# Cross-attention with an FFN on one core: V computed straight in rows for two head groups at once, and a slot's value products in one piece

## Chip, cores, metric

One NeuronCore of one Trainium2 chip runs the whole kernel in one launch. The metric is the device time of the launch in microseconds (us), median over runs. TensorE (PE in the rows) multiplies, VectorE (DVE), ScalarE (ACT) and GpSimd (POOL) work element by element, SyncE (SP) issues most DMAs.

## The reference, cut

For 32 batches of 64 rows of width 512, with H = 32 query heads, 8 key/value heads (groups), D = 128:

```python
q = (layernorm(x) @ Wq).reshape(nb, 64, 32, 128)     # k, v likewise from ctx, with 8 heads
q, k = rope(q), rope(k)                              # cos/sin rows gathered by position
k, v = repeat(k, 4), repeat(v, 4)                    # 4 query heads share a group
attn = softmax(where(mask == 0, -1e9, q @ k.T / sqrt(128)))
x = x + (attn @ v).reshape(nb, 64, 4096) @ Wo
# FFN: router softmax over 8 experts gives in_scale and out_scale per row
xf = layernorm(x)
x = x + (xf * in_scale @ sign(weight).T * out_scale + bias)
```

All inputs and results are float32. The kernel keeps that precision on TensorE by splitting each operand into a part `hi`, rounded to fp32r, and the rest `lo`, and multiplies hi·hi + hi·lo + lo·hi: three matmuls for each product of 128 rows.

## The kernel before

**Slots.** The 2048 rows make 16 tiles of 128 rows (two batches), taken in 4 quarters of 4 tiles (512 columns when transposed). For each quarter the 8 groups follow one another. A slot does, at the same time, the projections of its own group U (K, four Q heads, V: `project(s, 0..5)`), the attention of the group before (scores, softmax, values) and the output projection of the group before that (`out_proj(s, 0..3)`, one for each tile). There are 32 such slots (slot 0 only projects, slot 1 has no output projection), then `attend_last` and a last stage. Beside this, some slots take in a tile of the next quarter (transposes of context, positions and x: an *intake* slot; g = 2 to 5 of the first quarter, g = 0, 1, 6, 7 of the second and third), and slots g = 2 to 5 of the later quarters run the FFN of a finished tile (an *FFN* slot). What is neither is a *plain* slot. Of the even slots 2 to 30, six are FFN slots, six intake slots, three plain.

**Order.** Every engine runs its own list, written out by hand (`slot(s)` in each engine's block); semaphores tie them. Nothing is scheduled by a planner. A projection is 12 matmuls with 512 columns moving (`split_products`, L1129: 4 chunks of 128 by three products), the weights stationary. TensorE's order in a slot before: `out_proj 0`, V's transposes, scores, `out_proj 1, 2, 3`, `project 0`, transposes of the probabilities (`probs_T`), `project 1`, `values 0`, `project 2`, `project 3`, `values 1`, `project 4`, `project 5`, with the small steps of intake and FFN between them.

**V before.** `project(s, 5)` gives V of the group transposed (columns are rows of the context). ScalarE copies it to `vT` (`v_out`, L605); in the next slot `v_rows` (L1161) turns it with four TensorE transposes into `V_BANK`, ScalarE and VectorE split it into `v_hi` (`v_in_rows`, L571) and `v_lo` (`v_lo_split`, L846).

**Values.** `values(s, d)` (L1192) multiplies V with the transposed probabilities of two tiles (a *duo*): 12 matmuls of 64 rows by 256 columns, always two at a time in the two halves of the array. Both duos write the same two banks `o_ps`, so `values 1` waits until `out_hi` (ScalarE) and `out_lo` (VectorE) have emptied them, and stands two projections later.

**Weights.** A group's K, Q, V and Wo chunks (10 in a slot, 256 KB each) come through a ring of five raw buffers in the order `STREAM`; ScalarE makes `hi` (`split_hi`, L553), GpSimd makes `lo` (`split_lo`, L413), and `wsplit_lo` counts them. `w_hi`, `w_lo` hold three chunks (`WRING`).

**Rotary embedding.** After a projection j (0 is K, 1 to 4 are Q heads) VectorE's `rotate(s, j)` (L860) makes two half products with sin into `swp` and one with cos, and GpSimd's `rope_sum(s, j)` (L424) adds them. `cos_done` frees the PSUM bank of the projection, `roped` lets the scores of the next slot begin.

Of the kernel before, what the change touches and what calls it, by code (L numbers as in the profile page):

```python
# [26 lines left out]
def attention_ffn(nc, x, ctx_in, pos, mask, wq, wk, wv, wo, ffn_w, ffn_bias, gate_w, in_scale, out_scale,  # L27
# [26 lines left out]
    STREAM = [0, 1, 2, 3, 6, 4, 7, 5, 8, 9]  # L54
    FIRST_STREAM = [0, PROJ - 1, 1, 2, 3, 4]
# [11 lines left out]
    with stack:  # L67
# [16 lines left out]
        vT = sb("vT", [P, BT])  # L84
        v_hi, v_lo = (sb(n, [P, PAIRS, D], F32R) for n in ("v_hi", "v_lo"))
# [5 lines left out]
        pT_hi, pT_lo = (sb(n, [P, 2, 2 * P], F32R) for n in ("pT_hi", "pT_lo"))  # L91
# [6 lines left out]
        c_tile, x_tile, f_tile, fT = (sb(n, [P, E]) for n in ("c_tile", "x_tile", "f_tile", "fT"))  # L98
# [22 lines left out]
        xs_hi, xs_lo = sb("xs_hi", [P, E], F32R), sb("xs_lo", [P, E], F32R)  # L121
# [4 lines left out]
        in_raw, out_raw, gate_raw = probs[:, 0, :], probs[:, 1, :], c_tile  # L126
# [3 lines left out]
        sc_ps, tr_ps, aux = (stack.enter_context(nc.psum_tensor(n, [P, 512], F32)) for n in ("sc_ps", "tr_ps", "aux"))  # L130
        o_both = stack.enter_context(nc.psum_tensor("o_ps", [P, 2, 512], F32))
        o_ps = [o_both[:, i, :] for i in range(2)]

        DUO_BANK, V_BANK, TABLE_BANK = [sc_ps, tr_ps], o_ps[0], o_ps[1]
        C_BANK, X_BANK = [aux, sc_ps, tr_ps, o_ps[0]], [chunk[2], o_ps[1], sc_ps, aux]
        ROWS_BANK, SGN_BANK, GATE_BANK = [tr_ps, o_ps[0]], [o_ps[0], sc_ps, tr_ps, aux], o_ps[1]
        x_first = [x_tile, f_tile, fT, y]
# [28 lines left out]
        PROJ_BANK = [1, 2, 0, 1, 2, 1]  # L166
# [16 lines left out]
        vT_ok, v_tr, v_h, v_ok = sem("vT_ok"), sem("v_tr"), sem("v_h"), sem("v_ok")  # L183
# [21 lines left out]
        class Slot:  # L205


            def __init__(self, q, g, ffn, intake, residual=False):
                self.q, self.g = q, g
                self.U = q * KVH + g  # L210
# [8 lines left out]
                self.ffn, self.intake, self.residual = ffn, intake, residual  # L219
                side = q % 2  # L220
# [10 lines left out]
        def run_slots(eng, slot, last_step, newest_first=False):  # L231


            quarter(eng, slot, 0, False, True)
            with eng.Fori(1, QT - 1) as q:
                quarter(eng, slot, q, True, True)
            quarter(eng, slot, QT - 1, True, False)
            slot(last_attention)
            last_slot = Slot(QT, 1, False, False)
            for turn in range(PAIRS + LAST_STEPS - 1):  # L240
                tiles = [p for p in range(PAIRS) if 0 <= turn - p < LAST_STEPS]
                if newest_first or turn < PAIRS:
                    tiles.reverse()
                else:
                    tiles.sort(key=lambda p: turn - p == PRODUCT_STEP)
                for p in tiles:
                    last_step(last_slot, turn - p, p)

        def quarter(eng, slot, q, has_ffn, has_intake):
# [5 lines left out]
            with eng.Fori(TJ, TJ + PAIRS) as g:  # L255
                slot(Slot(q, g, has_ffn, first, has_intake))
            with eng.Fori(TJ + PAIRS, KVH) as g:
                slot(Slot(q, g, False, has_intake and not first))
# [5 lines left out]
        def jobs_of(s):  # L264
# [3 lines left out]
            t = tile_in(s, i if s.residual else s.g if isinstance(s.g, int) else s.g - PAIRS) if s.intake else None  # L268
# [3 lines left out]
        def loads_of(s):  # L272

            return FIRST_STREAM if s.first_proj else STREAM if s.proj else [PROJ + h for h in range(HG)]

        def ring_use(s, n):

            return (n % RING, n // RING + 1) if s.first_proj else ((n - HG) % RING, 2 * s.U + (n - HG) // RING + 1)

        def split_count(s, n):  # L280

            return n + 1 if s.first_proj else s.U * CH - HG + n + 1

        def rank(s, j):

            return FIRST_STREAM.index(j) if s.first_proj else j

        def proj_bank(s, j):

            return chunk[0 if s.first_proj and j == PROJ - 1 else PROJ_BANK[j]]  # L290
# [19 lines left out]
        def heads_of_o(p):  # L310
            return o_both[:, :, bass.ts(p % 2, HG * S)].rearrange("p b (h s) -> p b h s", h=HG)
# [9 lines left out]
        def flat2(buffer):  # L321
            return buffer[:, :, :].rearrange("p b n -> p (b n)")
# [9 lines left out]
        def _(sp):  # L332
            def load_tile(t):

                sp.wait_ge(c_tr, t)
                sp.dma_start(c_tile[:, :], row_of(ctx_t, t)).then_inc(c_in, 16)
                sp.wait_ge(x_tr, t)
                sp.dma_start(x_tile[:, :], row_of(x_t, t)).then_inc(x_in, 16)

            def load_weights(s):  # L340
                for n, c in enumerate(loads_of(s)):
                    r, _ = ring_use(s, n)
                    if c >= PROJ:
                        grp = (s.g + KVH - 1) % KVH if isinstance(s.g, int) else s.g - 1
                    else:
                        grp = s.g
                    if not (s.first_proj and n < RING):
                        sp.wait_ge(wsplit_lo, split_count(s, n) - RING)
                    if c < PROJ:
                        src = (wk_c[:, :, bass.ts(grp, D)] if c == 0 else  # L350
                               wv_c[:, :, bass.ts(grp, D)] if c == PROJ - 1 else
# [4 lines left out]
                    if s.first_proj and n == 0:  # L356
# [21 lines left out]
            def slot(s):  # L378
                if s.intake:
                    load_tile(jobs_of(s)[0][0])  # L380
# [20 lines left out]
        def _(pool):  # L401
# [11 lines left out]
            def split_lo(s, n):  # L413
# [3 lines left out]
                if c < PROJ:  # L417
                    hi, lo = (flat(w[:, rank(s, c) % WRING, :, :]) for w in (w_hi, w_lo))
# [39 lines left out]
            def first_projections(s):  # L458
                second = Slot(0, 1, False, False)
                for n in range(3, PROJ):  # L460
                    split_lo(s, n)
                    rope_sum(s, n - 3)
                split_lo(second, 0)
                rope_sum(s, KQ - 2)
                split_lo(second, 1)
                rope_sum(s, KQ - 1)

            def slot(s):
# [13 lines left out]
                if s.proj:  # L482
                    split_lo(s, 3)
                    split_lo(s, 4)
                    rope_sum(s, 0)
                    rope_sum(s, 1)
                    split_lo(s, 5)
                    split_lo(s, 6)
                    split_lo(s, 7)
                    rope_sum(s, 2)  # L490
                if s.ffn:
                    xs_lo_split(f[0], in_slot)
                if s.proj:
                    rope_sum(s, 3)
                    split_lo(s, 8)
                    split_lo(s, 9)
                    rope_sum(s, 4)
# [29 lines left out]
            def first_quarter():  # L527
# [4 lines left out]
                split_lo(first, 0)  # L532
                split_lo(first, 1)
                pool.wait_ge(consts, 1)
                pool.wait_ge(x_st3, PAIRS)
                nc.gpsimd.tensor_tensor(s_rstd[:, :], s_var[:, :], half[:, :], ALU.pow).then_inc(x_st4, PAIRS)
                split_lo(first, 2)
                wait_alone(pool, rows_tr, PAIRS)
                nc.gpsimd.memset(scores[:, :, :], MASKED).then_inc(fill_ok, 1)

# [5 lines left out]
        def _(act):  # L546
# [6 lines left out]
            def split_hi(s, n):  # L553
# [3 lines left out]
                if c < PROJ:  # L557
                    k = rank(s, c)
                    if not (s.first_proj and k < WRING):
                        act.wait_ge(proj_done, s.U * PROJ + k - WRING + 1)  # L560
                    hi = flat(w_hi[:, k % WRING, :, :])
# [9 lines left out]
            def v_in_rows(s):  # L571
                act.wait_ge(v_tr, s.U)
                if not s.first_attn:
                    act.wait_ge(pv_done, (s.U - 1) * DUOS)
                copy(flat2(v_hi), V_BANK[:, :]).then_inc(v_h, 1)

            def exp_duo(s, d, part=range(8)):
# [3 lines left out]
                if not s.first_attn:  # L581
                    act.wait_ge(probs_tr, n - 1)
# [6 lines left out]
            def pT_hi_split(s, d):  # L589
# [3 lines left out]
                if not (s.first_attn and d == 0):  # L593
                    act.wait_ge(pv_done, n)
                copy(flat2(pT_hi), DUO_BANK[d][:, :]).then_inc(pT_h, 1)
# [8 lines left out]

            def v_out(s):  # L605
                act.wait_ge(proj_done, s.U * PROJ + rank(s, PROJ - 1) + 1)
                if not s.first_proj:
                    act.wait_ge(v_tr, s.U)
                copy(vT[:, :], proj_bank(s, PROJ - 1)[:, :]).then_inc(vT_ok, 1)
# [847 lines left out]
```

## Time and profile before

| | us |
|---|---|
| median of 3 runs (1177.56 to 1177.73) | 1177.7 |
| the profiled execution, its own time | 1177.43 |
| its span on the core | 1175.6 |
| TensorE busy in the span | 1159.1 (99%) |
| VectorE / GpSimd / ScalarE busy | 802.8 / 707.3 / 552.3 |
| granted TensorE clock, mean | 0.994 |

TensorE has work nearly all the time, and 95% of the chain of work that ended last lies on it. Busy times of matmuls overlap one another (a 512-column product shows 0.39 us, but starts follow each other faster), so TensorE's time is read from start to start in the timeline and not from the durations. A wait is worth something only where TensorE itself stands still for it.

### The profile page before, as it was taken

The numbers are of one execution on the slowest core, as the hardware profiler recorded it, in microseconds if no ns is written. First come the engines' busy times: TensorE is split into PE (matmuls) and PEld (weight loads), VectorE is DVE, ScalarE is ACT, GpSimd is POOL, SyncE is SP. The second block draws the span as 40 slices with busy tenths as digits, with TensorE's granted clock in tenths as the row PEclk, the third lists the DMA queues.
The fourth block names the chain that finished last, engine by engine and source line by source line (L and its number), as shares of the span: only waits on it lengthen the run. The fifth ranks groups of instructions, "written<-read, shape, count | busy, mean of one in ns | idle before, by whom it ended". The sixth has DMA issues, their size and how long they took to land.

```text
span 1175.6 us, 23824 instructions
## 1 busy us (share of the span) xinstructions
PE 1159.1 (99%) x7684; PEld 953.9 (81%) x7684; DVE 802.8 (68%) x1359; ACT 552.3 (47%) x1768; POOL 707.3 (60%) x589
## 2 busy tenths in 40 slices
PE   8999999999999999999999999999999999999996
PEld 7788888888888888888888888888888888888875
DVE  6876676676676666677676666776667676666664
ACT  4554454445544354454444453544444354444442
POOL 5755566655557665566655576655567565676525
PEclk9999999999999999999999999999999999999997
DMA  8322433233223223343322232332333222222200
GB/s 237 99 87 85 119 120 98 66 95 105 77 73 107 72 79 97 96 112 107 99 75 71 82 107 78 91 104 78 87 100 90 63 80 65 86 90 82 71 1 37
DMA packets 136348, 104.99 MB, mean 89 GB/s; under 512 B 12712, under 2 KB 111016, under 8 KB 136288
## 3 DMA queue, kind: packets, MB, share of 16 engines
q1 hardware_dynamic: 128848, 93.72, 27.5%
q10 hardware_dynamic: 6672, 8.40, 2.2%
q0 software_dynamic: 768, 2.10, 0.6%
q8 instruction: 34, 0.56, 0.2%
q14 instruction: 26, 0.21, 0.1%
HBM read 100.00 MB, written 4.19 MB: 89 GB/s over the span
## 4 chain that ended last, share of the span: by engine, by line
PE 95%; DVE 1%; POOL 1%; ACT 1%; issue 1%; DMA 1%; POOLq 0%; ACTq 0%; DVEq 0%
PE chunk L1133 25%; PE chunk L1134 24%; PE chunk L1135 24%; PE o_ps L1206 5%; PE sc_ps L1181 3%; PE tr_ps L1181 2%; PE aux L1122 2%; PE o_ps L1122 2%; PE tr_ps L1122 1%; PE sc_ps L1122 1%; PE aux L1286 1%; PE aux L1287 1%; PE aux L1260 1%; DMA qT<-in_ctx 1%; PE aux L1272 0%
## 5 line engine op out<-in xcount | busy, mean ns | idle before, releaser
L422 POOL TENSOR_TENSOR w_lo<-raw,w_hi 128x512 fp32r<-128x512 f32 x192 | 247.3, 1300 | 373.7 <-ACT w_hi L548 373.6
L876 DVE TENSOR_TENSOR swp<-chunk,sinT 64x512 f32<-64x512 f32 x320 | 220.3, 688 | 99.4 <-PE chunk L1135 95.3
L1133 PE MATMUL chunk<-xT_hi,w_hi 128*128 128x512 f32 (+1 forms) x512 | 208.9, 408 | 0.6 <-POOL w_lo L422 0.6
L1134 PE MATMUL chunk<-xT_lo,w_hi 128*128 128x512 f32 (+1 forms) x512 | 200.8, 392 | 0.0
L1135 PE MATMUL chunk<-xT_hi,w_lo 128*128 128x512 f32 (+1 forms) x512 | 200.1, 391 | 0.0
L1133 PE MATMUL chunk<-wo_hi,oT_hi 128*128 128x512 f32 x496 | 196.8, 397 | 1.2 <-POOL wo_lo L422 0.8
L1135 PE MATMUL chunk<-wo_hi,oT_lo 128*128 128x512 f32 x496 | 193.7, 390 | 0.0
L1134 PE MATMUL chunk<-wo_lo,oT_hi 128*128 128x512 f32 x496 | 193.2, 390 | 0.0
L429 POOL TENSOR_TENSOR qT<-qT,swp 128x512 f32<-128x512 f32 x128 | 167.2, 1306 | 40.0 <-DVE qT L878 38.0
L584 ACT ACTIVATE probs<-scores,neg_max 128x64 f32<-128x64 f32 x512 | 170.4, 335 | 27.3 <-DVE neg_max L833 27.3
L818 DVE TENSOR_TENSOR acc<-chunk,acc 128x512 f32 (+1 forms) x128 | 88.2, 689 | 137.3 <-PE chunk L1135 136.8
L422 POOL TENSOR_TENSOR wo_lo<-raw,wo_hi 128x512 fp32r<-128x512 f32 x124 | 159.3, 1297 | 4.8 <-ACT wo_hi L548 4.8
L548 ACT ACTIVATE w_hi<-raw 128x512 fp32r<-128x512 f32 x192 | 117.8, 629 | 61.3 <-issue 46.8
L1133 PEld LDWEIGHTS chunk<-xT_hi,w_hi 128*128 128x128 f32 x512 | 96.9, 189 | 23.2 <-issue 0.8
L1135 PEld LDWEIGHTS chunk<-xT_hi,w_lo 128*128 128x128 f32 x512 | 96.2, 188 | 21.6
L1133 PEld LDWEIGHTS chunk<-wo_hi,oT_hi 128*128 128x128 f32 x496 | 93.1, 188 | 22.1 <-issue 1.8
L1134 PEld LDWEIGHTS chunk<-xT_lo,w_hi 128*128 128x128 f32 x512 | 96.4, 188 | 17.4
L1135 PEld LDWEIGHTS chunk<-wo_hi,oT_lo 128*128 128x128 f32 x496 | 93.1, 188 | 20.2
L1134 PEld LDWEIGHTS chunk<-wo_lo,oT_hi 128*128 128x128 f32 x496 | 93.3, 188 | 18.0
L1133 PE MATMUL chunk<-cT_hi,w_hi 128*128 128x512 f32 (+1 forms) x256 | 100.0, 391 | 0.8 <-POOL w_lo L422 0.8
L1135 PE MATMUL chunk<-cT_hi,w_lo 128*128 128x512 f32 (+1 forms) x256 | 99.9, 390 | 0.0
L1134 PE MATMUL chunk<-cT_lo,w_hi 128*128 128x512 f32 (+1 forms) x256 | 99.8, 390 | 0.0
(281 smaller groups left out, 1907.9 us busy)
## 6 DMA issues: line engine op xcount, KB each, us to landing
raw<-in_L_xattn_Wq SPq DMA_DIRECT2D x128, 256.0 KB, 2.8
raw<-in_L_xattn_Wo SPq DMA_DIRECT2D x128, 256.0 KB, 2.7
raw<-in_L_xattn_Wk SPq DMA_DIRECT2D x32, 256.0 KB, 4.6
raw<-in_L_xattn_Wv SPq DMA_DIRECT2D x32, 256.0 KB, 3.0
acc<-in_x ACTq DMA_DIRECT2D x14, 256.0 KB, 2.9
c_tile<-in_ctx SPq DMA_DIRECT2D x12, 256.0 KB, 2.9
x_tile<-in_x SPq DMA_DIRECT2D x12, 256.0 KB, 3.4
result<-y ACTq DMA_DIRECT2D x12, 256.0 KB, 2.0
```

The source lines that it names most:

```text
L422: nc.gpsimd.tensor_tensor(lo, raw[:, r, :], hi.bitcast(F32), ALU.subtract).then_inc(wsplit_lo, 1)
L429: nc.gpsimd.tensor_tensor(dst, dst, by_batch(swp[:, j % 2, :]), ALU.add).then_inc(roped, 1)
L548: return nc.scalar.activation(dst, src, ACT.Copy)
L584: last = nc.scalar.activation(probs[:, d, bass.ts(k, S)], scores[:, 2 * d + k // 4, bass.ts(k % 4, S)], ACT.Exp, bias=neg_max[:, d, k:k + ...
L818: nc.vector.tensor_tensor(a, chunk[OUT_BANK[p]][:, :], a, ALU.add).then_inc(added, 1)
L876: last = nc.vector.tensor_tensor(swp[to, k, :], bank[of, :], sinT[to, here], ALU.mult)
L1122: return nc.tensor.transpose(dst, src, ident[:, :])
L1133: nc.tensor.matmul(bank, a_hi, b_hi, start=i == 0, stop=False)
L1134: nc.tensor.matmul(bank, a_hi, b_lo, start=False, stop=False)
L1135: last = nc.tensor.matmul(bank, a_lo, b_hi, start=False, stop=i == n - 1)
L1181: last = nc.tensor.matmul(DUO_BANK[d][a * S:(a + 1) * S, bass.ts(place, S)], qT[:, hp, queries], kT[:, bass.ts(at, S)], start=True, stop=True)
L1206: last = nc.tensor.matmul(o_both[:, b, bass.ts(i, HG * S)], v[keys, 2 * d + i, :], probs_of[keys, i, :], start=k == 0, stop=k == 2)
```

## The change

V is no longer projected transposed. In every even slot, `v_rows(s, 0)` and `v_rows(s, 1)` take the context as the stationary operand (128 rows of it at a time) and the weights of V for this group and the next as the moving one, 2 x 128 = 256 columns: 4 tiles x 4 chunks x 3 products = 48 matmuls for two groups, in place of two times 12 matmuls of 512 columns. The result stands in rows, so `vT`, its copy and the four transposes of each slot go. An even slot loads 11 weight chunks (V of the next group too), an odd one 9. `values 0` and `values 1` follow each other directly: the second duo writes `duo_ps`, the two banks that the scores and the transposed probabilities of both duos use, and the split probabilities have a buffer for each duo. The scores therefore wait for all four `out_lo` of the slot before. To make room, the FFN's tiles share buffers with the intake (`f_tile` is `x_tile`, `fT` is `c_tile`, `xs_hi`, `xs_lo` are the first duo's split probabilities). The orders of all engines are rewritten for even and odd slots, the quarters are written out one after another, and the start computes V of groups 0 and 1 before x is transposed.

```diff
-    STREAM = [0, 1, 2, 3, 6, 4, 7, 5, 8, 9]
-    FIRST_STREAM = [0, PROJ - 1, 1, 2, 3, 4]
+    V_OWN, V_NEXT = PROJ - 1, CH
+    EVEN_STREAM = [0, 1, 2, 3, 6, 4, 7, V_OWN, V_NEXT, 8, 9]
+    ODD_STREAM = [0, 1, 2, 3, 6, 4, 7, 8, 9]
+    FIRST_STREAM = [0, V_NEXT, V_OWN, 1, 2, 3, 4]
...
-            def v_rows(s):
-
-                pe.wait_ge(vT_ok, s.U)
-                if not s.first_attn:
-                    pe.wait_ge(o_lo, (s.U - 1) * PAIRS)
-                for p in range(PAIRS):
-                    last = transpose(V_BANK[:, bass.ts(p, D)], vT[:, bass.ts(p, P)])
-                last.then_inc(v_tr, 1)
+            def v_rows(s, i):
+
+                if i == 0:
+                    pe.wait_ge(wsplit_lo, split_count(s, max(loads_of(s).index(c) for c in (V_OWN, V_NEXT))))
+                    if not s.first_proj:
+                        pe.wait_ge(cos_done, s.U * KQ + 4)
+                elif not s.first_proj:
+                    pe.wait_ge(o_lo, (s.U - 1) * PAIRS + 2)
+                lowest = min(entry(s, V_OWN), entry(s, V_NEXT))
+                both = slice(lowest, WRING, 1 if s.first_proj else 2)
+                for t in range(2):
+                    here = span(s.side * BT + (2 * i + t) * P, P)
+                    bank = v_bank(s, i)[:, bass.ts(t, 2 * D)].rearrange("p (g d) -> p g d", g=2)
+                    for c in range(EC):
+                        nc.tensor.matmul(bank, cT_hi[:, c, here], w_hi[:, both, c, :], start=c == 0, stop=False)
+                        nc.tensor.matmul(bank, cT_hi[:, c, here], w_lo[:, both, c, :], start=False, stop=False)
+                        last = nc.tensor.matmul(bank, cT_lo[:, c, here], w_hi[:, both, c, :], start=False, stop=c == EC - 1)
...
             def values(s, d):
...
-                else:
-                    pe.wait_ge(o_lo, 2 * n)
...
-                            last = nc.tensor.matmul(o_both[:, b, bass.ts(i, HG * S)], v[keys, 2 * d + i, :], probs_of[keys, i, :],
+                            last = nc.tensor.matmul(OUTPUTS[d][:, b, bass.ts(i, HG * S)], v[keys, 2 * d + i, s.odd, :], probs_of[keys, d, i, :],
...
             def slot(s):
...
-                    values(s, 0)
+                project(s, 1 if s.odd else 2)
+                values(s, 0)
+                values(s, 1)
                 if s.ffn:
                     t_route(f, in_slot)
-                if s.proj:
-                    project(s, 2)
+                project(s, 2 if s.odd else 3)
                 if s.ffn:
                     t_in_scales(f, in_slot)
-                if s.proj:
-                    project(s, 3)
-                if s.attn:
-                    values(s, 1)
+                project(s, 3 if s.odd else 4)
                 if s.ffn:
                     t_out_scales(f, in_slot)
-                if s.proj:
+                if s.odd:
                     project(s, 4)
+                else:
+                    v_rows(s, 0)
                 if s.ffn:
                     t_product(f, in_slot)
-                if s.proj:
-                    project(s, 5)
+                if not s.odd:
+                    v_rows(s, 1)
```

In an even slot TensorE's order is now: `out_proj 0, 1`, scores, `out_proj 2, 3`, `project 0, 1`, `probs_T`, `project 2`, `values 0, 1`, `project 3, 4`, `v_rows 0, 1`. In an odd slot: `out_proj 0`, scores, `out_proj 1, 2, 3`, `project 0`, `probs_T`, `project 1`, `values 0, 1`, `project 2, 3, 4`.

TensorE in slot 24 (even), from the end of `out_proj 0`; `wo` and `oT` are the output projection, `sc_ps` or `duo_ps` take the scores. Before:

```order
L1135 MATMUL chunk<-wo_hi,oT_lo 128x512
L1122 MATMUL o_ps<-ident,vT 128x128 [waits o_lo,vT_ok]
L1122 MATMUL o_ps<-ident,vT 128x128 x3
L1181 MATMUL sc_ps<-kT,qT 64x64 [waits pT_l,roped]
L1181 MATMUL sc_ps<-kT,qT 64x64 x15
```

Now, in the same slot, the end of `project 4` and the start of V's products; before, `project 5` and its 12 products `chunk<-cT,w` stood here:

```order
L1167 MATMUL chunk<-xT_hi,w_hi 128x512
L1168 MATMUL chunk<-xT_lo,w_hi 128x512
L1169 MATMUL chunk<-xT_hi,w_lo 128x512
L1211 MATMUL chunk<-w_hi,cT_hi 128x256 [waits cos_done,wsplit_lo]
L1212 MATMUL chunk<-w_lo,cT_hi 128x256
L1213 MATMUL chunk<-w_hi,cT_lo 128x256
```

The transposes are gone, and the 256-column products wait for the last two weight splits and for a rotation.

GpSimd in slot 24: `w_lo` are the splits of K, Q and V chunks, `wo_lo` those of Wo, `kT` and `qT` the rope sums. Before:

```order
L422 TENSOR_TENSOR w_lo<-raw,w_hi 128x512 [waits wsplit_hi] x4
L422 TENSOR_TENSOR wo_lo<-raw,wo_hi 128x512 [waits wsplit_hi]
L429 TENSOR_TENSOR kT<-kT,swp 128x512 [waits cos_done,sin_done]
L429 TENSOR_TENSOR qT<-qT,swp 128x8x64 [waits cos_done,sin_done]
L422 TENSOR_TENSOR w_lo<-raw,w_hi 128x512 [waits wsplit_hi]
L422 TENSOR_TENSOR wo_lo<-raw,wo_hi 128x512 [waits wsplit_hi]
L422 TENSOR_TENSOR w_lo<-raw,w_hi 128x512 [waits wsplit_hi]
L429 TENSOR_TENSOR qT<-qT,swp 128x8x64 [waits cos_done,sin_done] x2
```

Now:

```order
L455 TENSOR_TENSOR w_lo<-raw,w_hi 128x512 [waits wsplit_hi] x4
L455 TENSOR_TENSOR wo_lo<-raw,wo_hi 128x512 [waits wsplit_hi]
L462 TENSOR_TENSOR kT<-kT,swp 128x512 [waits cos_done,sin_done]
L455 TENSOR_TENSOR w_lo<-raw,w_hi 128x512 [waits wsplit_hi]
L462 TENSOR_TENSOR qT<-qT,swp 128x8x64 [waits cos_done,sin_done]
L455 TENSOR_TENSOR wo_lo<-raw,wo_hi 128x512 [waits wsplit_hi]
L455 TENSOR_TENSOR w_lo<-raw,w_hi 128x512 [waits wsplit_hi] x2
L462 TENSOR_TENSOR qT<-qT,swp 128x8x64 [waits cos_done,sin_done]
```

The `w_lo` row marked x2 holds the splits of both V chunks; it stands behind the first two rope sums (`kT`, `qT`) and two other splits.

VectorE in slot 24, from the second half of the softmax; `swp` and then `kT` or `qT` are a rotation, `pT_lo` splits the transposed probabilities, `oT_lo` is `out_lo`. Before:

```order
L843 TENSOR_TENSOR probs<-probs,srec 128x512 [waits recd]
L876 TENSOR_TENSOR swp<-chunk,sinT 64x512 [waits roped,proj_done,scores_done]
L876 TENSOR_TENSOR swp<-chunk,sinT 64x512
L878 TENSOR_TENSOR kT<-chunk,cosT 128x512
L811 TENSOR_TENSOR pT_lo<-sc_ps,pT_hi 128x512 [waits pT_h]
```

Now (these rows stand the same in an odd slot):

```order
L873 TENSOR_TENSOR probs<-probs,srec 128x512 [waits recd]
L841 TENSOR_TENSOR pT_lo<-duo_ps,pT_hi 128x512 [waits pT_h] x2
L907 TENSOR_TENSOR swp<-chunk,sinT 64x512 [waits roped,proj_done,scores_done]
L907 TENSOR_TENSOR swp<-chunk,sinT 64x512
L909 TENSOR_TENSOR kT<-chunk,cosT 128x512
```

The rotation of K, which came ahead of the first `pT_lo`, now comes behind both.

## Rows read from the trace of the kernel before

**Rows 1.** The page's first part: busy time, share of the span, instructions

```profile
span 1175.6 us, 23824 instructions
...
PE 1159.1 (99%) x7684; PEld 953.9 (81%) x7684; DVE 802.8 (68%) x1359; ACT 552.3 (47%) x1768; POOL 707.3 (60%) x589
```

**Rows 2.** TensorE's timeline, slot 14 (start us, duration us, line, out<-in, count)

```profile
482.87 0.39 PE L1135 MATMUL chunk<-wo_hi,oT_lo 128*128 128x512 f32 x1
483.10 0.60 PE L1122 MATMUL o_ps<-ident,vT 128*128 128x128 f32 x4
483.63 1.15 PE L1181 MATMUL sc_ps<-kT,qT 128*64 128x64 f32 x32
```

**Rows 3.** The same timeline around the transposes of the probabilities

```profile
497.07 0.60 PE L1122 MATMUL sc_ps<-ident,probs 128*128 128x128 f32 x4
497.50 0.60 PE L1122 MATMUL tr_ps<-ident,probs 128*128 128x128 f32 x4
...
498.51 0.48 PE L1133 MATMUL chunk<-xT_hi,w_hi 128*128 x1
```

**Rows 4.** The same timeline around the first value products

```profile
501.12 0.39 PE L1135 MATMUL chunk<-xT_hi,w_lo 128*128 x1
501.44 0.38 PE L1206 MATMUL o_ps<-pT_hi,v_hi 64*128 64x256 f32 x2
501.67 0.28 PE L1206 MATMUL o_ps<-pT_lo,v_hi 64*128 64x256 f32 x2
...
502.13 0.28 PE L1206 MATMUL o_ps<-pT_hi,v_lo 64*128 64x256 f32 x2
502.34 0.50 PE L1133 MATMUL chunk<-xT_hi,w_hi 128*128 x1
502.68 0.40 PE L1134 MATMUL chunk<-xT_lo,w_hi 128*128 x1
```

**Rows 5.** TensorE's timeline, slot 13 (FFN): 21 starts of 512-column products, and 8-column products

```profile
452.58 0.39 PE L1133 MATMUL chunk<-wo_hi,oT_hi 128*128 128x512 f32 x1
...
457.34 0.39 PE L1133 MATMUL chunk<-cT_hi,w_hi 128*128 x1
...
460.94 0.96 PE L1260 MATMUL aux<-gateT,fT 128*128 128x8 f32 x8
461.75 0.48 PE L1133 MATMUL chunk<-xT_hi,w_hi 128*128 x1
```

**Rows 6.** ScalarE's timeline, slot 14

```profile
497.70 0.60 ACT L548 ACTIVATE pT_hi<-sc_ps 128x512 fp32r<-128x512 f32 x1 [3.41 <-PE sc_ps L1122]
...
503.01 1.08 ACT L548 ACTIVATE oT_hi<-o_ps 128x512 fp32r<-128x512 f32 x2
```

**Rows 7.** VectorE's timeline, slot 14

```profile
503.06 0.69 DVE L878 TENSOR_TENSOR qT<-chunk,cosT 128x512 f32<-128x512 f32 x1
503.67 0.68 DVE L811 TENSOR_TENSOR pT_lo<-tr_ps,pT_hi 128x512 fp32r<-128x512 f32 x1
504.27 1.28 DVE L811 TENSOR_TENSOR oT_lo<-o_ps,oT_hi 128x512 fp32r<-128x512 f32 x2
505.58 1.39 DVE L876 TENSOR_TENSOR swp<-chunk,sinT 64x512 f32<-64x512 f32 x2
507.00 0.69 DVE L878 TENSOR_TENSOR qT<-chunk,cosT 128x512 f32<-128x512 f32 x1
```

**Rows 8.** GpSimd's timeline, slot 14

```profile
503.90 1.30 POOL L429 TENSOR_TENSOR qT<-qT,swp 128x512 f32<-128x512 f32 x1
505.16 1.29 POOL L422 TENSOR_TENSOR w_lo<-raw,w_hi 128x512 fp32r<-128x512 f32 x1
```

**Rows 9.** The start: TensorE's first product of the first Q projection

```profile
23.05 0.39 PE L1133 MATMUL chunk<-xT_hi,w_hi 128*128 128x512 f32 x1
```

**Rows 10.** The start: GpSimd's last gather of rope rows, and the gathers' median to landing

```profile
11.18 0.95 POOL L403 DMA_INDIRECT scores<-rope_table,pos_first  x1 [0.30 <-issue]
...
scores<-rope_table,pos_first POOLq DMA_INDIRECT x4, 5.6
```

More of the change, by code:

```diff
@@ L89, in attention_ffn @@
         probs = sb("probs", [P, DUOS, 8 * S])
-        pT_hi, pT_lo = (sb(n, [P, 2, 2 * P], F32R) for n in ("pT_hi", "pT_lo"))
+        pT_hi, pT_lo = (sb(n, [P, DUOS, 2, 2 * P], F32R) for n in ("pT_hi", "pT_lo"))
         swp = sb("swp", [P, 2, BT])
@@ L219, in __init__ @@
                 self.ffn, self.intake, self.residual = ffn, intake, residual
+                self.past_ffn = intake and isinstance(g, int) and g >= TJ
                 side = q % 2
@@ L231, in run_slots @@
         def run_slots(eng, slot, last_step, newest_first=False):
[L234 to L237, printed above, removed]
+            for q in range(QT):
+                quarter(eng, slot, q, q > 0, q < QT - 1)
             slot(last_attention)
@@ L254, in quarter @@
             slot(Slot(q, 1, False, has_intake and not first))
[L255 to L258, printed above, removed]
+            with eng.Fori(0, PAIRS // 2) as pair:
+                slot(Slot(q, pair * 2 + TJ, has_ffn, first, has_intake, odd=0))
+                slot(Slot(q, pair * 2 + TJ + 1, has_ffn, first, has_intake, odd=1))
+            slot(Slot(q, KVH - 2, False, has_intake and not first))
+            slot(Slot(q, KVH - 1, False, has_intake and not first))
         def tile_in(s, i):
@@ L592, in pT_hi_split @@
                 act.wait_ge(probs_tr, n + 1)
-                if not (s.first_attn and d == 0):
-                    act.wait_ge(pv_done, n)
-                copy(flat2(pT_hi), DUO_BANK[d][:, :]).then_inc(pT_h, 1)
+                if not s.first_attn:
+                    act.wait_ge(pv_done, n - DUOS + 1)
+                copy(flat(pT_hi[:, d, :, :]), DUO_BANK[d][:, :]).then_inc(pT_h, 1)
             def out_hi(s, p):
@@ L984, in slot @@
                     return first_attention(s)
+                if s.first_proj:
+                    for j in range(1, KQ):
+                        rotate(s, j)
+                    return scales_lo()
+                if s.odd:
+                    even = Slot(s.q, s.g - 1, False, False, odd=0)
+                    v_lo_split(even, 0)
+                    v_lo_split(even, 1)
                 if s.intake:
@@ L1148, in out_proj @@
                     pe.wait_ge(cos_done, (s.U - 1) * KQ + 3)
+                elif p == 1 and s.odd:
+                    pe.wait_ge(v_ok, s.U)
                 elif p == 1:
-                    pe.wait_ge(vT_ok, s.U)
+                    pe.wait_ge(cos_done, (s.U - 1) * KQ + 4)
                 else:
@@ L1303, in first_projections @@
             def first_projections(s):
-                for j in (5, 1, 2, 3, 4):
+                for j in range(1, KQ):
                     project(s, j)
@@ L1343, in slot @@
                     t_f(f, in_slot)
[L1344 removed]
+                if s.odd:
                     out_proj(s, 1)
[L1346 to L1352 removed]
+                out_proj(s, 2)
+                out_proj(s, 3)
+                project(s, 0)
+                if not s.odd:
+                    project(s, 1)
+                probs_T(s, 0)
+                probs_T(s, 1)
                 if s.intake:
```

378 lines of the change are left out of this document (194 added, 184 removed).

## The prediction
> **What bounds the kernel.** I read the page's busy shares first: TensorE is busy 1159.1 of 1175.6 us, GpSimd 60%, VectorE 68% [rows 1]. So the end is set by what TensorE has to issue, and a change counts in two ways: matmul time taken off or put on, and new stands of TensorE at a wait. Then I read TensorE's timeline from start to start, since the durations overlap. A stream of 512-column products starts 21 times between 452.58 and 457.34, one each 0.2267 us [rows 5]. The page hides that small pieces cost more than their columns: around the first value products [rows 4] the last start of the projection is 501.12, so its successor was due at 501.35; the products start at 501.44, 0.09 late, their second pair comes 0.23 later, the next ones every 0.117 (four in 501.67 to 502.13), and the next projection begins at 502.34 with a first step of 0.34 in place of 0.227. Last I read one slot on VectorE, ScalarE and GpSimd for the pace of the work that feeds TensorE.
>
> **1. V's transposes go.** In slot 14 the four transposes start at 483.10 and the scores at 483.63, 0.53 us later [rows 2]. Four transposes in a row take 0.43 [rows 3]; the other 0.10 is like the 0.09 by which the value products come late after a projection [rows 4], and the scores will probably still pay it. I take 0.43 for each of 32 slots: **-13.8 us** (bounds 0.43 to 0.53, so down to -17.0).
>
> **2. Value products in one piece.** One block now takes 502.34 - 501.35 = 0.99, and the projection behind it loses 0.11 on its first step and some 0.05 on the next ones: 1.15 [rows 4]. Its six pairs alone are 6 x 0.117 = 0.70. A second block right behind the first should cost 0.70 in place of 1.15, so 0.45 in each of slots 1 to 31: 14.0. In the 12 FFN slots the output-scale product, which followed the second block, now stands alone between large products and pays about 0.1 more: **-12.8 us**. If the second block pays its own slow first pair again (0.11), it is -9.4.
>
> **3. 48 products of 256 columns for 24 of 512.** No row has 128 rows x 256 columns. Below: half of 0.2267, that is 0.1134, no loss. Above: a weight load that isn't hidden at all. What a load costs is seen where almost nothing moves: eight 8-column products take 461.75 - 460.94 = 0.81, 0.10 each [rows 5]; 0.10 + 0.113 = 0.213 then. Nearest are the pairs of value products, two loads and two times 256 columns in 0.117 [rows 4]. Their loads are of 64 rows, but in the 512-column stream full loads are hidden too: 0.2267 leaves no room for a 0.10 load beside the columns. I take 0.118: 48 x 0.118 = 5.66 against 24 x 0.2267 = 5.44, +0.22 for each of 16 pairs of groups: **+3.6 us** (0 to +76).
> The row says that a 512-column product costs 13 ns more than 512 steps of 2.4 GHz (213 ns). The Trainium skill, "TensorE: Matmul & The Clock Gate", section "Back-to-back issue gap", gives N/2.4 + 2.5 ns for a single product, thus an estimated 109 ns at 256 columns; by it part 3 would be -3 us. The 0.2267 of this trace stands above that formula's 216, so I stay with the rows.
>
> **4. A new wait in even slots.** V's products wait for the splits of both V chunks and for the rotation of project 3 (`cos_done`). I follow one plain even slot from T, the start of the first transposes of probabilities.
> TensorE: two times 0.435 for the transposes, project 2 with its slow first step 2.84, value blocks 0.99 + 0.70, projects 3 and 4 together 5.62: V's products could start at **T + 11.0** [rows 3 to 5].
> The others: ScalarE's `pT_hi` starts 0.63 after the transposes (497.70 against 497.07), takes 0.60, the second follows 0.5 later and ends at T + 1.73 [rows 3, 6]. VectorE steps every 0.60 [rows 7], so two `pT_lo` end their turn at T + 2.46, and only then K's rotation runs: two sin halves 1.42 (505.58 to 507.00), cos 0.69 [rows 7], done at T + 4.57. GpSimd starts the sum about 0.14 later (503.75 to 503.90) [rows 7, 8] and steps every 1.26 [rows 8]: sum K, a Q split, sum Q, a Wo split, V, V; the sixth ends at T + 12.3, and with 0.1 to pass it on TensorE starts at **T + 12.4**: 1.4 us of standing. The rotations alone (K, Q1, one `out_lo`, Q2, Q3 at 2.02 and 0.60) reach T + 11.3, so GpSimd is the later one. In an intake slot TensorE has 0.57 more to do and the wait is 0.9. In an FFN slot it has router steps of some 1.6 us, V's products come after the splits, but the output scales wait for VectorE's `scale_in` behind rotation Q3: 0.3. Three plain, six intake and six FFN slots: 3 x 1.4 + 6 x 0.9 + 6 x 0.3 = **+11.4 us** (0 to some 25).
> What is behind that wait stays covered. GpSimd still has two sums and two splits after the V splits, done by T + 18.5; the next scores come 5.66 + 2.72 after T + 12.4, at T + 20.8. The odd slot's own chain (sums until T + 17.4) ends before the next scores at T + 19.2. The loads follow the splits in the same ring, and an even slot's three later ones have 3 us and more before their use. The softmax starts earlier than before, since neither V's copy nor its split stands ahead of it.
>
> **5. Start and slot 2.** One split now stands ahead of the last two gathers: the last starts at 11.18 + 1.26 = 12.44 and lands 5.6 later [rows 10], at 18.0. TensorE transposes the rows (0.9), runs V's 48 products (5.7) and x's 16 transposes (1.7), until 26.3; ScalarE's and VectorE's splits behind that take the first Q projection to 28.4, against 23.05 [rows 9]. V of group 1 (12 x 0.2267 = 2.7) is then done already: +2.6. In slot 2 the first output projection follows the value products directly and waits for two copies and one split of them, about +1.4. **+4.0 us** (0 to +6).
>
> **At nothing:** the copies of V on ScalarE and VectorE (as many as before, off the path); the second buffer of split probabilities; the shared FFN and intake tiles (their waits end a slot ahead of the use); the loads, the same number of chunks in all; the longer program.
>
> **Sum:** -13.8 - 12.8 + 3.6 + 11.4 + 4.0 = **-7.6 us** on the profiled execution's 1177.43, whose time is 0.27 below the median: 1169.8, and as a median **1170.0 us**.
>
> **Rivals.**
> (a) *The even slots don't wait.* If the sums and splits reach V's chunks 1.4 us sooner than I chain them, part 4 is gone: 1158 to 1159. For it: GpSimd is 60% busy and stood idle before the splits. Against: the chain hangs on a rotation that now starts after both `pT_lo`, and its paces are read off directly. 0.20.
> (b) *The chain is longer: slower.* Place: the same wait. Each 0.1 us more in an even slot is 1.5 us, so from 0.5 us more (a plain wait of 1.9) the gain is used up. ScalarE now makes two weight splits ahead of `pT_hi`; were `pT_hi` held up by two of them (0.54 each by the copies' pace [rows 6]), every even slot would wait 1.1 longer: 1170 + 16 = 1186. Against: in an even slot their projection is done 2.7 us before T. 0.13.
> (c) *The weight loads of V's products are seen: slower.* At 0.128 us for each (10 ns more) the kernel is where it was; with the load not hidden at all (0.213) it is 1170 + 73 = 1243. For it: twice as many loads for the same columns. Against: rows 4 and 5, as above. The Trainium skill has this rule in the same page, "What overlaps and what doesn't": a weight load overlaps a running product only where the row groups differ; here they are the same 128 rows. The 512-column stream of this trace speaks against it. 0.07.
> (d) *The value blocks or transposes give less than read* (the second block pays its lead-in, the scores a longer one): 1175 to 1178. 0.05.
>
> **How the numbers follow.** Forecast with its own spread 1160 to 1177: 0.55; (a) 0.20, (b) 0.13, (c) 0.07, (d) 0.05. The range 1155 to 1182 takes in (a), most of the forecast and (d), and the nearer part of (b); what it leaves out is (c), the far part of (b) and of (a). About 0.2%, 2.4 us, is what a measurement of this kernel can tell from no change: 1175.3 to 1180.1. Forecast and (a) lie below but for a little: faster 0.76; part of (d) and of (b) within: 0.08; the rest slower: 0.16.
>
> **What would show it.** In the profile after: no transposes of vT; one run of 24 value products for a slot; starts of the 256-column products 0.118 apart; idle of TensorE ahead of the first of them, some 1.4, 0.9 and 0.3 us in plain, intake and FFN even slots, ended by GpSimd's `w_lo` (by `scale_in` in the last); the first Q projection near 28 us. If the products are 0.13 or more apart, or the idle time is another engine's or above 2 us, the forecast is wrong at that step; if TensorE shows no idle there, (a) holds.

## The result and the profile after

The changed kernel takes 1189.57 us (median of 4 runs, 1188.14 to 1193.1), the kernel before beside it 1177.72: the ratio is 1.0104, with a 95% interval of 1.0085 to 1.0123. It is slower by 1%, where 0.7% less had been forecast. The profiled execution took 1189.76 us.

The first part of the page after, against [rows 1]:

```profile
span 1187.9 us, 22903 instructions
...
PE 1142.3 (96%) x7932; PEld 959.9 (81%) x7932; DVE 819.0 (69%) x1359; ACT 534.1 (45%) x1736; POOL 708.2 (60%) x589
```

TensorE is busy 16.8 us less in a span that is 12.3 us longer: it idles 45.6 us in place of 16.5. VectorE, with as many instructions as before, is busy 16.2 us longer. The view of waits names where TensorE stands (waited for, us in total, times, longest). Before, two of its rows, the longest one (in the last stage) and projections that wait for a split:

```profile
PE aux L1272 <- DVE cT_hi L811: 3.5, 1, 3.5
...
PE chunk L1133 <- POOL w_lo L422: 1.4, 2, 0.8
```

After:

```profile
PE aux L1327 <- DVE c_tile L969: 10.2, 6, 1.7
PE chunk L1211 <- POOL w_lo L455: 10.0, 9, 1.4
PE aux L1320 <- DVE cT_hi L841: 3.5, 1, 3.5
PE aux L1156 <- DVE route L959: 3.5, 6, 0.6
...
PE chunk L1167 <- DVE qT L909: 2.2, 1, 2.2
```

L1211 is V's first product, which waits for its weight split: forecast 9.6 us in nine slots, measured 10.0. L1327, the output scales of even FFN slots, waits 1.7 us for `scale_in` (forecast 0.3). L1156, the transposes of the routing in odd FFN slots, was not thought to wait at all. Read from start to start in TensorE's timeline (first product of one slot's `out_proj 0` to that of the next; mean, us):

| pair of slots (even and odd) | before | after | measured | forecast |
|---|---|---|---|---|
| 3 plain | 66.30 | 66.34 | +0.04 | -0.14 |
| 6 intake | 68.57 | 68.15 | -0.42 | -0.64 |
| 6 FFN | 74.01 | 75.45 | +1.44 | -1.04 |

Slot 2 starts 5.0 us later (60.6, now 65.6), and what follows slot 31 takes 1.0 more. The forecast had +3.3 (the 4.0 of part 5, less 0.7 for parts 1 to 3 in slot 1) and -0.4 there. So 14.9 of the 19.9 us by which the span missed lie in six FFN pairs. Most of that comes from one small instruction. The view of VectorE's lines for `route` (min/median/max in ns), before and after:

```profile
L928 DVE TENSOR_SCALAR route<-rexp,rrec x12: 234/235/236, 352.2 to 1031.5; 128x24 f32<-128x24 f32 x12
```

```profile
L959 DVE TENSOR_SCALAR route<-rexp,rrec x12: 1356/1360/1365, 360.3 to 1047.5; 128x24 f32<-128x24 f32 x12
```

The same 24 columns take 1.36 us in place of 0.235, all twelve times. The trace before held a sign of it, under another tile name. In its last stage the same line runs four more times:

```profile
L928 DVE TENSOR_SCALAR swp<-rows x4: 235/832/1302, 1146.3 to 1159.5; 128x24 f32<-128x24 f32 x4
```

In its timeline the short one (0.235) has GpSimd idle; the three long ones (0.67, 0.99 and 1.30) each end 0.03 us after GpSimd's addition of the bias. VectorE's timeline and GpSimd's in slot 13 (an odd FFN slot) after:

```profile
474.24 0.69 DVE L909 TENSOR_TENSOR kT<-chunk,cosT 128x512 f32<-128x512 f32 x1
474.85 0.15 DVE L957 RECIPROCAL rrec<-rsum 128x1 f32<-128x1 f32 x1
475.04 1.36 DVE L959 TENSOR_SCALAR route<-rexp,rrec 128x24 f32<-128x24 f32 x1
476.42 1.39 DVE L907 TENSOR_TENSOR swp<-chunk,sinT 64x512 f32<-64x512 f32 x2
```

```profile
475.08 1.28 POOL L462 TENSOR_TENSOR kT<-kT,swp 128x512 f32<-128x512 f32 x1 [2.08 <-DVE kT L909]
```

The end of K's rotation releases GpSimd's sum of K; the multiply of `routing` stands right behind that rotation (only a reciprocal of 0.15 us lies between) and ends 0.04 us after the sum. Before, in the same slot, GpSimd was idle until the multiply was done (VectorE, then GpSimd):

```profile
463.24 0.23 DVE L928 TENSOR_SCALAR route<-rexp,rrec 128x24 f32<-128x24 f32 x1
```

```profile
463.53 1.29 POOL L422 TENSOR_TENSOR w_lo<-raw,w_hi 128x512 fp32r<-128x512 f32 x1 [9.67 <-ACT w_hi L548]
```

In the even FFN slot 12 after, TensorE's timeline shows the price at `scale_in`, and then V's products:

```profile
445.32 0.50 PE L1327 MATMUL aux<-out_sc,routeT 128*128 128x512 f32 x1 [1.66 <-DVE c_tile L969]
445.66 0.28 PE L1211 MATMUL chunk<-w_hi,cT_hi 128*128 128x256 f32 x1
445.77 0.28 PE L1212 MATMUL chunk<-w_lo,cT_hi 128*128 128x256 f32 x1
...
448.53 0.40 PE L1334 MATMUL aux<-sgnT,pT_hi 128*128 128x512 f32 x1
```

Here 24 of V's products take 448.53 - 445.66 = 2.87, 0.120 each, close to half of the 0.2267 of a 512-column product [rows 5]: their weight loads are hidden.

The last stage has a new wait too, at the scores of `attend_last`. Its row in the view of waits after, for which the view before has none:

```profile
PE duo_ps L1231 <- POOL qT L462: 1.5, 1, 1.5
```

### The profile page after: what moved, and what is told of

It reads as the page before. It is cut to its first block, busy times and chain, and to the rows that moved or that the text cites. A ratio compares the mean times of both kernels' runs of the same rounds, so it can differ in the third digit from the quotient of the medians.

```text
span 1187.9 us, 22903 instructions
## 1 busy us (share of the span) xinstructions
PE 1142.3 (96%) x7932; PEld 959.9 (81%) x7932; DVE 819.0 (69%) x1359; ACT 534.1 (45%) x1736; POOL 708.2 (60%) x589
## 4 chain that ended last, share of the span: by engine, by line
PE 75%; DVE 11%; issue 5%; POOL 5%; ACT 2%; DMA 1%; ACTq 0%; POOLq 0%; DVEq 0%
PE chunk L1167 18%; PE chunk L1169 18%; PE chunk L1168 18%; PE duo_ps L1231 5%; DVE swp L907 4%; POOL w_lo L455 2%; PE aux L1156 2%; PE chunk L1211 1%; DVE pT_lo L841 1%; PE duo_ps L1156 1%; PE o_ps L1213 1%; PE o_ps L1212 1%; PE o_ps L1211 1%; PE chunk L1213 1%; PE chunk L1212 1%
## 5 line engine op out<-in xcount | busy, mean ns | idle before, releaser
L1167 PE MATMUL chunk<-xT_hi,w_hi 128*128 128x512 f32 x512 | 207.1, 405 | 4.3 <-DVE qT L909 2.2
L1169 PE MATMUL chunk<-xT_hi,w_lo 128*128 128x512 f32 x512 | 200.8, 392 | 0.0
L1168 PE MATMUL chunk<-xT_lo,w_hi 128*128 128x512 f32 x512 | 200.2, 391 | 0.0
L848 DVE TENSOR_TENSOR acc<-chunk,acc 128x512 f32<-128x512 f32 x128 | 87.3, 688 | 82.6 <-PE chunk L1169 82.2
L841 DVE TENSOR_TENSOR pT_lo<-duo_ps,pT_hi 128x512 fp32r<-128x512 f32 x64 | 41.3, 686 | 115.8 <-ACT pT_hi L593 115.8
L462 POOL TENSOR_TENSOR kT<-kT,swp 128x512 f32<-128x512 f32 x32 | 41.3, 1292 | 93.4 <-DVE kT L909 93.4
L630 ACT ACTIVATION_READ_ACCUMULATOR probs<-scores,neg_max 128x1 f32 x512 | 96.8, 189 | 0.0
```

The lines of the kernel that those rows point to most:

```text
L462: nc.gpsimd.tensor_tensor(dst, dst, by_batch(swp[:, j % 2, :]), ALU.add).then_inc(roped, 1)
L630: last = nc.scalar.activation(probs[:, d, bass.ts(k, S)], scores[:, 2 * d + k // 4, bass.ts(k % 4, S)], ACT.Exp, bias=neg_max[:, d, k:k + ...
L841: return nc.vector.tensor_tensor(dst, src, hi.bitcast(F32), ALU.subtract)
L848: nc.vector.tensor_tensor(a, chunk[OUT_BANK[p]][:, :], a, ALU.add).then_inc(added, 1)
L1167: nc.tensor.matmul(bank, a_hi, b_hi, start=i == 0, stop=False)
L1168: nc.tensor.matmul(bank, a_hi, b_lo, start=False, stop=False)
```

## Experiments

All ratios are against the kernel before, on one chip for each group. The changed kernel itself was timed only four times, 1188.1 to 1193.1, so a difference from it of some 2 us (e2_scale, e3_stream, e4_start) is not clear of its spread, and there the trace decides. Theory A: routing's multiply and GpSimd's sum exclude one another, and the 1.1 us are on the path. Theory B: `scale_in` stands too late, whatever the multiply does. Theory C: the multiply is long of itself in the changed kernel.

**e1_route: routing between the halves of K's rotation.**

```diff
-                rotate(s, 0)
+                rotate(s, 0, (lambda: routing(f[0], in_slot)) if s.ffn else None)
...
-                if s.ffn:
-                    routing(f[0], in_slot)
```

`rotate` calls it after its two sin products, ahead of the cos product.

> Base is the changed kernel (1189.6 us); in FFN slots routing's multiply (route<-rexp,rrec) moves on VectorE from behind K's rotation to between the sin and cos halves of it, where GpSimd stands idle. Theory A (the two exclude each other): in the changed kernel the multiply starts within 0.05 us of GpSimd's sum of K and ends with it, 1.36 us in place of 0.235 in all 12 FFN slots; moved, it should take 0.24 again, TensorE's wait for the routing transposes in odd slots (0.58) should go and the wait for scale_in ahead of the output scales in even slots fall from 1.7 to about 0.55: 6 x (0.58 + 1.12) = 10.2 us, about 1179.5. Theory B (scale_in's place behind rotation Q3 alone costs the wait): the multiply gets short, the time stays within 2 us of 1189.6. Theory C (the multiply is long of itself in this kernel, because its tiles lie elsewhere): it stays at 1.36 us, and so does the time.

Measured: 1179.7 us (ratio 1.0021, 1.0012 to 1.0031), 9.9 less than the changed kernel. The view of lines, and the wait that is left:

```profile
L961 DVE TENSOR_SCALAR route<-rexp,rrec x12: 233/235/239, 360.6 to 1037.8; 128x24 f32<-128x24 f32 x12
```

```profile
PE aux L1327 <- DVE c_tile L971: 4.3, 6, 0.7
```

The row of the routing transposes is gone. FFN pairs are 1.78 us shorter, the others are as they were. Theory A holds to 0.2 us; B and C fall.

**e2_scale: scale_in ahead of rotation Q3 in even slots, routing left alone.**

```diff
                     rotate(s, 2)
-                    rotate(s, 3)
                     if s.ffn:
                         scale_in(f[0], in_slot)
+                    rotate(s, 3)
```

> Base is the changed kernel (1189.6 us); in even FFN slots scale_in stands ahead of rotation Q3 instead of behind it, routing stays where it is. Theory A: scale_in comes 2.0 us earlier and the output scales no longer wait, but rotation Q3 ends 0.6 later, and V's products, which need it, start at best 0.35 us earlier than now: 6 x 0.35 = 2 us, about 1187.5, with a wait of TensorE for rotation Q3. Theory B: the whole wait of 1.7 us in six slots goes, about 1179.6.

Measured: 1188.81 us (1.0099, 1.0083 to 1.0114), 0.8 less. The wait for `scale_in` is gone and V's products stand instead:

```profile
PE chunk L1211 <- DVE qT L909: 8.7, 6, 1.5
```

Even FFN slots are 0.24 us shorter, 1.4 in all. VectorE's list is late as a whole, and the order of these two steps behind the long multiply hardly matters. A had 2 us, so a size is off, but B had 10.

**e3_stream: V's chunks ahead of the second Wo chunk.**

```diff
-    EVEN_STREAM = [0, 1, 2, 3, 6, 4, 7, V_OWN, V_NEXT, 8, 9]
+    EVEN_STREAM = [0, 1, 2, 3, 6, 4, V_OWN, V_NEXT, 7, 8, 9]
```

In even slots ScalarE also makes the split of `V_NEXT` behind `out_hi` 2 and 3.

> Base is the changed kernel (1189.6 us); in even slots the two V chunks come one place earlier in the stream of weights, ahead of the second chunk of Wo, so that GpSimd makes their splits one step (1.26 us) earlier. If the wait ahead of V's products hangs on GpSimd's list as the prediction chained it, plain slots keep some 0.2 to 0.3 us of 1.4 (then rotation Q3 ends it) and intake slots none of 0.9: 3 x 1.1 + 6 x 0.9 = 8.7 us, about 1181. Rival: the hi split of the second V chunk, which waits for the end of project 3, or rotation Q3 ends the wait nearly as late: under 3 us, 1187 or more. FFN slots unchanged in both.

Measured: 1187.19 us (1.0079, 1.0065 to 1.0092), 2.4 less: the rival. Read from slot to slot, plain even slots are 0.6 and intake slots 0.3 us shorter, 3.5 in all. GpSimd's row is gone, and the next one stood close behind it:

```profile
PE chunk L1214 <- DVE qT L912: 6.7, 9, 0.8
```

Rotation Q3 ends the wait, 0.8 us after TensorE came, where the prediction had 0.3.

**e4_start: GpSimd's third Q split ahead of a rope sum in slot 0.**

```diff
                 split_lo(s, 4)
-                rope_sum(s, 1)
                 split_lo(s, 5)
-                rope_sum(s, 2)
+                rope_sum(s, 1)
                 split_lo(s, 6)
+                rope_sum(s, 2)
```

> Base is the changed kernel (1189.6 us); in slot 0 GpSimd makes the split of the third Q chunk ahead of the sum of the first Q head, not behind it. In the changed kernel TensorE stands 2.23 us ahead of the third Q projection (33.8 to 36.0), and the products after it start 0.43 apart for 3.5 us at a granted clock of 0.57 in place of 0.23, another 2.0 us. Theory A: both go, about 4.2 us, 1185.4, and the four Q projections of slot 0 take 10.9 us again in place of 15.2. Rival: the stand goes, the time comes back at the next wait (the scores' wait for the rope sum, slot 2's wait for out_lo): 1188 or more.

Measured: 1187.95 us (1.0091, 1.0075 to 1.0106), 1.6 less. In its trace the wait is gone, the four Q projections take 11.0 us in place of 15.2, and from their end to the start of slot 2 it takes 22.4 in both. Slots 2 to 31 take 1060.6 against 1060.7. So the place is Theory A's, and no later wait took the time back, as the rival has it; but the time itself (1187.95) is the rival's and not A's 1185.4. Two things of this trace that the edit does not touch took 1.9: the first Q projection began 0.8 later, and the last stage took 1.1 more (62.6 against 61.6), where TensorE was at the lower clock for longer. The stretch at half clock, some 1.6 of the 4.2, does not follow the stand in every execution either (last section). What the edit is worth over many runs stays open.

**e5_outlo: e1_route, and out_lo 0 behind rotation Q3 in even slots.**

```diff
-                    out_lo(s, 0)
                     rotate(s, 2)
                     rotate(s, 3)
                     if s.ffn:
                         scale_in(f[0], in_slot)
+                    out_lo(s, 0)
                     out_lo(s, 1)
```

> Base is the kernel of e1_route (1179.7 us); in even slots out_lo 0 moves on VectorE from ahead of rotation Q2 to behind rotation Q3 (and scale_in), nothing else. In e1_route the output scales still wait 0.7 us for scale_in in six even FFN slots, 4.3 us in all. If VectorE's list alone sets that wait, scale_in comes one out_lo (0.65 us) earlier: about 4 us, 1175.8, the row of the wait nearly gone. V's second half, which needs out_lo 0 and 1, starts 2.9 us behind the first and should not notice. In plain and intake slots nothing changes, since GpSimd's split of V ends the wait there (10.0 us stay). Rival: in FFN slots another wait takes its place at once (V's products for the splits or for rotation Q3): 1178 or more.

Measured: 1176.26 us (0.9987, 0.9978 to 0.9996), 3.4 less than e1_route. The row for `scale_in` is gone, and V's row stays as it was expected to:

```profile
PE chunk L1211 <- POOL w_lo L455: 9.9, 9, 1.4
```

**e6_all: the four edits together** (routing, stream, start, out_lo 0).

> Base is the changed kernel (1189.6 us) with four edits together: routing between the halves of K's rotation, V's chunks one place earlier in the stream, the third Q split ahead of a rope sum in slot 0, out_lo 0 behind rotation Q3. Measured apart they gave 9.9 (routing), 2.4 (stream) and 1.6 (start; 4.1 in slot 0 of its trace). The stream alone left a wait of 0.8 us for rotation Q3 in plain slots (6.7 us in nine); with out_lo 0 behind, Q3 ends 0.65 earlier, and GpSimd's split too, so plain and intake waits should fall to some 0.2 and 0: another 5 us. With 4 of e5_outlo: 9.9 + 2.4 + 3 + 5 + 4 = 24, about 1165. Then the forecast's gains are all there and its loss lay in the order of VectorE and GpSimd. Rival: the steps behind (scores waiting for rope sums or out_lo 3, the next slot's weights) come to bound it: 1172 or more.

Measured: 1163.68 us (0.9877, 0.9862 to 0.9893): 1.2% faster than the kernel before, the fastest of all. The page, and what is left of V's wait:

```profile
span 1162.7 us, 22903 instructions
...
PE 1141.3 (98%) x7932; PEld 960.7 (83%) x7932; DVE 804.1 (69%) x1359; ACT 534.3 (46%) x1736; POOL 707.7 (61%) x589
```

```profile
PE chunk L1214 <- POOL w_lo L455: 0.7, 3, 0.2
```

VectorE is back at 804.1 us. Even slots now take 35.68 (plain), 36.69 (intake) and 39.46 us (FFN), against 36.86, 37.57 and 41.32 in the changed kernel. The stream alone gave plain even slots 0.6, out_lo 0 alone nothing, both 1.2: two waits ended 0.6 apart.

**e7_before_sum: the kernel before, with the same collision put in.** In FFN slots GpSimd's sum of K moves ahead of two weight splits.

```diff
+                    if s.ffn:
+                        rope_sum(s, 0)
                     split_lo(s, 3)
                     split_lo(s, 4)
-                    rope_sum(s, 0)
+                    if not s.ffn:
+                        rope_sum(s, 0)
```

> Base is the kernel before (1177.4 us); in FFN slots GpSimd makes the sum of K ahead of the splits of the fourth and fifth chunk instead of behind them, so that it runs while routing's multiply starts. Theory A: the multiply, 0.235 us in the kernel before, starts some 0.6 us after the sum and lasts until the sum ends, 0.6 to 0.7 us, in all 12 slots; the time stays at 1177.4 within 0.2%, since VectorE then idles 1.4 us until the next projection. Theory C (the length belongs to the changed kernel's tiles): 0.235 us as before.

Measured: 1177.72 us (1.0, 0.9991 to 1.0009). The view of lines, then VectorE's and GpSimd's timelines in slot 13:

```profile
L931 DVE TENSOR_SCALAR route<-rexp,rrec x12: 693/697/721, 353.3 to 1033.1; 128x24 f32<-128x24 f32 x12
```

```profile
464.29 0.70 DVE L931 TENSOR_SCALAR route<-rexp,rrec 128x24 f32<-128x24 f32 x1
465.93 1.39 DVE L879 TENSOR_TENSOR swp<-chunk,sinT 64x512 f32<-64x512 f32 x2 [0.94 <-PE chunk L1138]
```

```profile
463.66 1.29 POOL L429 TENSOR_TENSOR kT<-kT,swp 128x512 f32<-128x512 f32 x1 [8.75 <-DVE kT L881]
```

The sum ends at 464.95, the multiply at 464.99, and so in all twelve slots (0.03 to 0.04 apart): it is the collision and not the changed kernel's tiles. It costs nothing here: VectorE still idles 0.94 us behind it.

**e8_values: e6_all with values 1 one projection later again.**

```diff
                 values(s, 0)
-                values(s, 1)
                 if s.ffn:
                     t_route(f, in_slot)
                 project(s, 2 if s.odd else 3)
+                values(s, 1)
```

> Base is the kernel of e6_all (1163.7 us); one part of the change is undone: values 1 stands one projection behind values 0 again, in slots 2 to 31. The prediction's part 2 gives 0.45 us for each: 30 x 0.45 = 13.5 us, about 1177. By its lower bound (the second block pays its own slow first pair when it stands right behind the first, 0.30 each) about 1173. Rival: the second duo's out_hi and out_lo come a projection later and the next slot's scores wait for them, 1 us or more in each slot: above 1190, with a row for that wait.

Measured: 1175.14 us (0.9981, 0.9972 to 0.999), 11.5 more than e6_all, between the 13.5 expected and its lower bound. By the timeline the piece is worth 0.5 in plain and intake slots, 0.39 in odd and 0.12 in even FFN slots. No new wait appears.

## Why the prediction was wrong

It forecast faster and the kernel got slower. By its own parts:

1. *V's transposes* and 2. *values in one piece*: right together. A plain odd slot, which has nothing else, fell from 33.19 to 29.48: -3.71. The two parts and V's old projection of 2.72, which is gone from it, make -3.60. Part 2 alone is 0.49 there (forecast 0.45). In the FFN slots e8_values shows 0.51 for a pair where the prediction took 0.70: 1.1 us in all.
3. *48 products of 256 columns*: 0.120 to 0.122 each, forecast 0.118: 0.1 to 0.2 more for a pair of groups, some 2 us in all. Rival (c) is refuted: nothing like 0.213. The Trainium skill, "TensorE: Matmul & The Clock Gate", section "Back-to-back issue gap", would have given an estimated 109 ns; the trace stands above it here as it did for 512 columns.
4. *The wait in even slots*: right in plain and intake slots, 10.0 us against 9.6. **The step that failed is "In an FFN slot ... the output scales wait for VectorE's scale_in behind rotation Q3: 0.3."** It measured 1.7, and 0.58 in the odd slots beside it. The chain was that of the trace before, with the multiply at its 0.235; but the change moved K's rotation to stand directly ahead of `routing`, so that the instruction which the rotation releases on GpSimd runs exactly when the multiply would. The prediction noted the move and costed only the rotation's delay. e1_route gives 9.9 us for this alone, half of the miss. The wait of 0.7 that is left (forecast 0.3) is what e5_outlo's 3.4 us come from. The price could have been seen: the row of `swp<-rows` above stood in the trace that the prediction was made from.
   The same part had rotation Q3 ready 0.3 us behind TensorE, and it was 0.8: rotations that follow one another directly start 2.14 apart (514.47 and 516.61 in slot 14), not 2.02, and in intake slots the prediction left x's split on VectorE (0.7) out of the chain. That wait was covered by GpSimd's, so it cost nothing until e3_stream took the cover away.
   Rival (b) named the right kind of thing, a longer chain ahead of the same wait, but put it on ScalarE's weight splits.
5. *The start*: the first Q projection came at 28.0 (forecast 28.4; the other traces with the same start have 28.4 to 30.3, so the trace's agreement to 0.4 is partly luck), but slot 2 started 1.7 later than forecast. The step "V of group 1 is then done already: +2.6" took the four Q projections behind it as unchanged; the third waited 2.2 for a split that GpSimd's new list puts behind a rope sum, and then ran at half clock (below). The row names a rotation of VectorE, which ended at 35.94; the split ended 0.06 before it, and e4_start, where the third projection follows the second without a gap, shows that the rotation is not needed. Together the four projections lost 4.2. It shows only as 1.7, since what follows up to slot 2 took about 2 us less than the forecast's parts make; why is not shown.

What followed slot 31 took 1.4 more than forecast. Part 4's step "The odd slot's own chain ... ends before the next scores at T + 19.2" failed there: an even slot has two output projections ahead of its scores, `attend_last` only one, so its scores come 2.72 earlier, at T + 16.4, ahead of the prediction's own T + 17.4. TensorE stood 1.5 us there for GpSimd's sum of the last Q head. This is read from the trace; no experiment moved it. The rest of the spread, 60.2 to 60.6 before and 61.5 to 62.7 in the changed kernel and its variants, lies mostly behind it. With the four edits the kernel lands at 1163.7, between the forecast of 1170 and rival (a)'s 1158: TensorE's savings were there, and VectorE's and GpSimd's lists gave them back.

## What to carry to other kernels

Where a change reorders two engines that release each other, lay both lists side by side at each small VectorE instruction that takes and gives SBUF tiles, and ask what GpSimd will be doing in that very moment, before a duration is taken over from the old trace. Look for the same line under every tile name there: a largest duration far above the smallest for one shape (1.30 against 0.235 us here) is a sign that it can wait. A wait that goes often has the next one just behind: it pays to read off both ends (here GpSimd's split and rotation Q3, 0.6 us apart) and move both. And where an engine had slack, the same collision costs nothing (e7_before_sum), so look first at whether the list is late.

## What the runs showed of the hardware

**VectorE's multiply waits for GpSimd.** The 24-column multiply of an SBUF tile by a column lasts 0.235 us with GpSimd idle, 0.70 when GpSimd's 1.29 us sum is half done, 1.36 when both start together; it ends 0.03 to 0.04 us after the sum each time. The last stage of the kernel before shows the same against another GpSimd instruction, the addition of the bias. The Trainium skill, "SBUF — State Buffer", section "Who interferes with whom", says that VectorE and GpSimd share one pair of SBUF ports under an exclusive lock, that `tensor_scalar` is among the instructions that can take it, and that the later one blocks fully; the traces agree. It also says that the first to issue wins. By the start stamps the multiply came 0.04 us earlier (475.04, 475.08; 0.04 in each of the twelve slots) and lost all the same, so stamps this close do not tell who wins. The runs show the waiting alone; that the ports are its cause is what the Trainium skill says.

**A 2.2 us stand can cost twice.** In slot 0 TensorE stood 2.23 us ahead of the third Q projection, after 5.4 us of products without a gap. Its timeline behind that, and the view of windows (window, length, busy us of PE, PEld, DVE, ACT, POOL, then the granted clock, DMA share, GB/s):

```profile
36.02 0.47 PE L1167 MATMUL chunk<-xT_hi,w_hi 128*128 128x512 f32 x1 [2.23 <-DVE qT L909]
...
37.04 0.63 PE L1167 MATMUL chunk<-xT_hi,w_hi 128*128 128x512 f32 x1
37.47 0.63 PE L1168 MATMUL chunk<-xT_lo,w_hi 128*128 128x512 f32 x1
```

```profile
36.00:40.00 4.00, 3.98 (x11) 3.15 (x12) 0.00 (x0) 0.00 (x0) 3.75 (x3) 0.57 0.35 78
```

Products start 0.43 apart instead of 0.23, the lower level of 1.2 GHz, until about 39.9: another 1.6 us. Without the stand, in e4_start, the same window is at full clock:

```profile
36.00:40.00 4.00, 4.00 (x19) 3.24 (x18) 2.80 (x5) 0.63 (x1) 3.67 (x4) 1.00 0.27 66
```

But the slow stretch does not follow each time. The same stand is in the traces of e1_route, e2_scale, e3_stream and e5_outlo; e2_scale has none of it:

```profile
37.20 0.47 PE L1167 MATMUL chunk<-xT_hi,w_hi 128*128 128x512 f32 x1 [2.23 <-DVE qT L909]
```

```profile
37.20:41.20 4.00, 4.00 (x17) 3.21 (x18) 0.93 (x2) 0.63 (x1) 3.80 (x3) 1.00 0.24 67
```

There the four Q projections take 13.6 us, against 15.2 with the slow stretch and 11.0 without the stand: the stand costs 2.5 us every time, the clock 1.6 more in four of five traces. The stand of 2.06 us ahead of the first Q projection was followed by such a stretch in two of eight traces (e3_stream, e8_values). Why the clock fell in some and not in others is not shown.
